# A four-layer graph network on one core: the edge grid of the preparing stage goes from 125 partitions of 800 steps to 128 partitions of 784 steps

## The chip, the cores and the metric

One Trainium2 chip, of which the kernel uses one core. The core has five engines: TensorE (PE; its weight loads are listed as PEld), VectorE (DVE), ScalarE (ACT), GpSimd (POOL) and SyncE (SP), each with an instruction queue of its own, and 16 DMA engines that all queues share. The engines meet through semaphores only. The metric is the device time of one execution in microseconds (us); lower is better.

## The reference, cut to what matters

There are 6250 nodes with 256 features and 100,000 edges. Each edge has a source, a destination, a type, a weight and a row of 128 attributes. The edges are given in order of destination. Four layers follow each other, each on the layer-normalised rows of the one before, each added to the running x:

```python
h = relu(layernorm(x)); x = x + L0(h, src, dst, edge_weight, ...)   # segment sum over src of (h@W)[dst]*weight
h = relu(layernorm(x)); x = x + L1(h, edge_index, edge_attr, ...)   # segment sum over src of edge_attr@W, in and out degrees
h = relu(layernorm(x)); x = x + L2(h, edge_index, edge_weight, ...) # attention over the edges of each dst, then a feed-forward
h = relu(layernorm(x)); x = x + L3(h, ..., src, dst, edge_type)     # segment sum over dst, then a GRU cell
```

So the edges are needed once grouped by source (layers 0 and 1) and once grouped by destination (layers 2 and 3).

## The kernel before

The kernel runs stages one after the other: `prepare`, `source_sums`, `layers_0_and_1`, `attention`, `layer_2`, `relations_and_layer_3`. Only `prepare` is touched by the change. The later stages walk over tiles of 128 edges of a sorted list; for each of 832 tiles GpSimd gathers 128 rows of a DRAM table with an indirect DMA (lines 782, 1289 and 1905).

`prepare` sorts. It lays the edges out as a grid of `EP` partitions by `STEPS` steps (125 by 800, which is exactly 100,000). What it does, engine by engine:

- VectorE ranks the edges by the block of 128 nodes to which their source belongs (`rank("src")`): it counts each of 49 blocks over the whole grid (line 554), then walks through the grid in four segments of `SEG` = 200 steps and writes each edge's place in the sorted list into `pos_src` (lines 572, 577, 583, 587). When a segment is done it raises `ranked_steps`. Then come the row statistics of x, a wait for GpSimd's `rstd` (line 663), the table of the tiles by source, the same ranking by destination, and the one-hots for the in-degrees (lines 689 and 691, a pair for each of the 800 steps), which TensorE sums (line 513). Its work on the grid ends with the copy of line 698.
- SyncE loads the edge attributes into `rec`, 8 steps (`HALF`) of all partitions at a time. `rec` has two halves, and half `h` is loaded again only when all 8 scatters out of it have landed (`rec_stored[h]`).
- ScalarE completes a half: it waits for the load (`rec_loaded[h]`) and the ranking, copies 8 columns of places into `pos_slot` (line 477) and four more fields into the records (line 478), and raises `rec_ready`.
- GpSimd writes the sorted records to DRAM: for each step one indirect DMA (a scatter, line 410) that takes one record of 132 floats (528 bytes) from each partition and writes it to the row of `src_records` that `pos_slot` names. So there is one scatter for each of the `STEPS`, 8 for a half, 16 for a turn of the loop. After the first 12 turns (`FIRST_PAIR`) GpSimd computes `rstd` (line 421), for which VectorE waits.

```python
gp.indirect_dma_start(out=src_records,
                      out_offset=bass.IndirectOffsetOnAxis(ap=pos_slot[:, k:k + 1], axis=0),
                      in_=rec[:, k, :], in_offset=None).then_inc(rec_stored[h], 16)
```

After its last scatter GpSimd waits until all have landed, copies the fields of the edges to DRAM tables (line 452), gathers them in windows of 128 (line 464), and `prepare` ends; `source_sums` begins with reading `src_records`.

Of the kernel before, what the change touches and what calls it, by code (L numbers as in the profile page):

```python
# [14 lines left out]
F32 = mybir.dt.float32  # L15
BF16 = mybir.dt.bfloat16
I32 = mybir.dt.int32
# [7 lines left out]
P = 128  # L25
NODES, D = 6250, 256
EDGES, ED = 100000, 128
BLOCKS = -(-NODES // P)
NODES_PAD = BLOCKS * P
LAST_ROWS = NODES - (BLOCKS - 1) * P  # L30
EP = 125
STEPS = EDGES // EP
UNROLL = 8
# [10 lines left out]
REC = ED + 4  # L44
# [127 lines left out]
def build(nc, A, OUT):  # L172
    with ExitStack() as whole:
# [20 lines left out]
        src_records = dram("src_records", (EDGES + P, REC))  # L194
        by_dst = {n: dram(f"by_dst_{n}", (EDGES + P, 1), F32 if n == "wgt" else I32)
# [31 lines left out]
def prepare(env):  # L227
# [3 lines left out]
    HALF = 8  # L231
    SEG = STEPS // 4
    SB = TURN_BLOCKS
    PAIRS = (BLOCKS - 1) // 2
    FIRST_PAIR = 12
    REC_TURNS = STEPS // (2 * HALF)
    with nc.cleanup_on_exit(), ExitStack() as ctx:
# [22 lines left out]
        iota_i = sb(ctx, "iota_i", [P, P], I32)  # L260
        pidx_i = sb(ctx, "pidx_i", [P, 1], I32)
# [66 lines left out]
        rel_pad = sem("x_pad")  # L328

        def grid(ap):  # L330
            return ap.rearrange("(p t) -> p t", t=STEPS)
# [3 lines left out]
        with nc.Block() as block:  # L335
            @block.sync
            def _(sp):
                sp.dma_start(key["src"][:], grid(A["src"])).then_inc(loaded_src, 16)
                sp.dma_start(key["dst"][:], grid(A["dst"])).then_inc(loaded_rest, 16)
                sp.dma_start(wgt[:], grid(A["edge_weight"])).then_inc(loaded_rest, 16)  # L340
                sp.dma_start(typ[:], grid(A["edge_type_16"])).then_inc(loaded_rest, 16)
                sp.dma_start(pair[:], A["dst"][STEPS - 1:STEPS - 1 + (EP - 1) * STEPS]
                             .rearrange("(p t) -> p t", t=STEPS)[:, 0:2]).then_inc(loaded_rest, 16)

                attr = A["edge_attr_128"].rearrange("(p t) d -> p t d", t=STEPS)

                def load(turn, h):
                    sp.dma_start(rec[:, h * HALF:(h + 1) * HALF, 0:ED],
                                 attr[:, bass.ds(turn * 2 * HALF + h * HALF, HALF), :]
                                 ).then_inc(rec_loaded[h], 16)  # L350

                for h in range(2):
                    load(0, h)
# [33 lines left out]
            def _(gp):  # L387
# [10 lines left out]
                gp.wait_ge(iotas, 7)  # L398
                nc.gpsimd.memset(ones_row[:], 1.0).then_inc(tail_ready, 1)
                gp.wait_ge(loaded_rest, 64)  # L400
# [56 lines left out]
                for ch in range(CHUNKS):  # L457
                    if ch:
                        gp.wait_ge(win_cast, ch)
                    for n, name in enumerate(("src", "dst", "wgt", "typ")):  # L460
                        w = windows[:, n, :]
                        if name == "wgt":
                            w = w.bitcast(F32)
                        gp.indirect_dma_start(out=w, out_offset=None, in_=by_dst[name],
                                              in_offset=bass.IndirectOffsetOnAxis(ap=start_i["dst"][:, ch:ch + 1], axis=0)
                                              ).then_inc(win_loaded, 16)

            @block.scalar
            def _(ac):

                def complete(turn):
# [15 lines left out]
                with ac.Fori(0, FIRST_PAIR) as turn:  # L487
                    complete(turn)
                ac.wait_ge(rstd_ready, 2)
                ac.wait_ge(loaded_x, 32)  # L490
                with ac.Fori(0, PAIRS) as pair_i:
                    complete(pair_i + FIRST_PAIR)
                    normalise(pair_i * 2)
                    normalise(pair_i * 2 + 1)
                normalise(BLOCKS - 1)
                with ac.Fori(FIRST_PAIR + PAIRS, REC_TURNS) as turn:
                    complete(turn)
# [30 lines left out]
            def _(ve):  # L528
                d = Counter(ve, dve)
                nc.vector.memset(X[:, BLOCKS - 1, :], 0.0).then_inc(rel_pad, 1)  # L530
# [10 lines left out]
                def rank(side, hi_t):  # L541

                    if side == "dst":
                        ve.wait_ge(loaded_rest, 64)
                    else:
                        ve.wait_ge(loaded_src, 16)
# [102 lines left out]

                ve.wait_ge(tail_ready, 2)  # L650
# [1487 lines left out]
```

## Time and profile before

| | us |
|---|---|
| median of 3 runs (5604.88 to 5611.56) | 5610.76 |
| the profiled execution, its device time | 5615.93 |
| its span from the first to the last instruction | 5614.1 |
| GpSimd's first scatter starts | 115.3 |
| GpSimd's last scatter starts | 1379.3 |
| VectorE's last operation on the grid starts | 1040.4 |
| first tile gather of the next stage starts | 1497.0 |

The span is the profiler's; the device time lies 1.8 us above it. Times in the rows further down are us from the span's start, and durations of single instructions are in ns where the row says so. "Idle before" a group is the time its engine stood still just before instructions of that group, with what ended it; "issue" means that nothing which the profile shows was waited for.

### The profile page before, as it was taken

The numbers are of one execution on the slowest core, as the hardware profiler recorded it, in microseconds if no ns is written. First come the engines' busy times: TensorE is split into PE (matmuls) and PEld (weight loads), VectorE is DVE, ScalarE is ACT, GpSimd is POOL, SyncE is SP. The second block draws the span as 40 slices with busy tenths as digits, with TensorE's granted clock in tenths as the row PEclk, the third lists the DMA queues.
The fourth block names the chain that finished last, engine by engine and source line by source line (L and its number), as shares of the span: only waits on it lengthen the run. The fifth ranks groups of instructions, "written<-read, shape, count | busy, mean of one in ns | idle before, by whom it ended". The sixth has DMA issues, their size and how long they took to land. (4 is left out here: it accounts for less than half of the span.)

```text
span 5614.1 us, 108115 instructions
## 1 busy us (share of the span) xinstructions
PE 3530.3 (63%) x16558; PEld 2634.7 (47%) x16559; DVE 3950.7 (70%) x14077; ACT 1757.7 (31%) x6303; POOL 3898.1 (69%) x4332
## 2 busy tenths in 40 slices
PE   0000035200277777776768999999989778888887
PEld 0000012100255555554547888888879644554444
DVE  9918999300477777774568888888868766666665
ACT  0000000000133333332337777777756411111111
POOL 2878887776477777775766666666647777676774
PEclk9999999999999999997879999999999889899998
DMA  2232233335355555554323333333322233333332
GB/s 75 76 84 79 76 82 88 87 88 125 76 156 157 157 158 155 157 157 93 94 86 96 94 94 94 95 94 95 94 66 66 88 111 114 103 110 106 108 108 78
DMA packets 491102, 578.41 MB, mean 103 GB/s; under 512 B 114758, under 2 KB 394328, under 8 KB 490945
## 3 DMA queue, kind: packets, MB, share of 16 engines
q0 software_dynamic: 189536, 397.34, 25.4%
q1 hardware_dynamic: 301473, 180.10, 11.8%
q14 instruction: 67, 0.55, 0.0%
q8 instruction: 26, 0.43, 0.0%
HBM read 491.28 MB, written 86.57 MB: 103 GB/s over the span
## 5 line engine op out<-in xcount | busy, mean ns | idle before, releaser
L410 POOL DMA_INDIRECT src_records<-rec,pos_slot x800 | 1005.0, 1256 | 345.2 <-issue 237.0
L1289 POOL DMA_INDIRECT a_row<-h_rows,a_idx x832 | 787.6, 947 | 369.8 <-PE a_p_s L1415 197.1
L1905 POOL DMA_INDIRECT r_row<-h_rows,r_idx x832 | 802.1, 964 | 310.2 <-issue 168.2
L782 POOL DMA_INDIRECT s_row<-h_rows,s_idx x832 | 794.5, 955 | 299.7 <-issue 171.7
L794 PE MATMUL s_sums<-s_row,s_hotw 128*128 128x256 f32 x1664 | 584.9, 434 | 329.8 <-DMA s_row<-h_rows,s_idx 231.7
L1946 PE MATMUL r_p_s<-r_row,r_hot 128*128 128x272 f32 x1664 | 602.2, 474 | 233.2 <-DVE r_row L2080 215.1
L1392 PE MATMUL a_p_q<-nodes,a_hotT 128*128 x1664 | 569.8, 424 | 55.5 <-DVE a_score L1459 54.1
L1946 PEld LDWEIGHTS r_p_s<-r_row,r_hot 128*128 128x128 f32 x1664 | 335.4, 221 | 516.8 <-DVE r_row L2080 233.8
L820 DVE TENSOR_TENSOR nodes<-nodes,s_sums 128x385 f32 x832 | 461.5, 555 | 157.1 <-PE s_sums L795 138.7
L1415 PE MATMUL a_p_s<-a_row,a_masked 128*128 128x257 f32 x1664 | 497.0, 380 | 2.1 <-DVE sums L1496 1.4
L794 PEld LDWEIGHTS s_sums<-s_row,s_hotw 128*128 128x128 f32 x1664 | 253.0, 192 | 477.1 <-issue 369.6
L2088 DVE TENSOR_TENSOR sums<-sums,r_p_s 128x272 f32 x832 | 358.6, 431 | 149.3 <-PE r_p_s L1946 103.2
L773 ACT ACTIVATE s_idx<-s_rec 128x1 int32<-128x1 f32 x832 | 167.9, 202 | 863.3 <-DMA s_rec<-src_records 731.3
L1496 DVE SCALAR_TENSOR_TENSOR sums<-sums,a_fade,a_p_s 128x257 f32 x832 | 399.3, 480 | 41.7 <-PE a_p_s L1415 3.7
L1459 DVE CUSTOM_DVE_ANT_0 a_prod<-a_p_q,a_row 128x258 f32<-128x258 f32 x832 | 353.5, 425 | 104.9 <-ACT a_masked L1338 63.3
L795 PEld LDWEIGHTS s_sums<-s_rec,s_hot 128*128 128x128 f32 x1664 | 323.0, 194 | 46.1
L477 ACT ACTIVATE pos_slot<-pos_src 125x8 int32 x100 | 20.9, 209 | 1014.8 <-DMA rec<-in_edge_attr 991.4
L1415 PEld LDWEIGHTS a_p_s<-a_row,a_masked 128*128 128x128 f32 x1664 | 314.5, 190 | 49.5 <-ACT a_masked L1359 2.3
L795 PE MATMUL s_sums<-s_rec,s_hot 128*128 128x129 f32 x1664 | 326.2, 278 | 0.0
L1338 ACT ACTIVATE a_masked<-a_far,a_score 128x128 f32<-128x128 f32 x832 | 323.7, 389 | 2.0 <-DVE a_score L1459 2.0
L1359 ACT ACTIVATE a_masked<-a_masked,a_mneg 128x128 f32<-128x128 f32 x832 | 324.2, 390 | 0.0
L504 PE MATMUL p_total<-cnt,ones 125*128 125x49 f32 x4 | 1.3, 432 | 492.2 <-DVEq L559 492.2
(308 smaller groups left out, 8747.5 us busy)
## 6 DMA issues: line engine op xcount, KB each, us to landing
s_rec<-src_records SPq DMA_DIRECT2D x832, 66.0 KB
rec<-in_edge_attr SPq DMA_DIRECT2D x100, 500.0 KB
s_row<-h_rows,s_idx POOLq DMA_INDIRECT x832
a_row<-h_rows,a_idx POOLq DMA_INDIRECT x832, 2.8
r_row<-h_rows,r_idx POOLq DMA_INDIRECT x832, 2.8
src_records<-rec,pos_slot POOLq DMA_INDIRECT x800
h_rows<-H SPq DMA_DIRECT2D x1, 6272.0 KB
x_rows<-nodes SPq DMA_DIRECT2D x49, 128.0 KB, 1.9
```

The costliest lines, as they stand in the source:

```text
L410: gp.indirect_dma_start(out=src_records, out_offset=bass.IndirectOffsetOnAxis(ap=pos_slot[:, k:k + 1], axis=0), in_=rec[:, k, :], in_offse ...
L782: gp.indirect_dma_start(out=row[:, k, :], out_offset=None, in_=env["h0_rows"], in_offset=bass.IndirectOffsetOnAxis(ap=idx[:, k:k + 1], axis=0)
L794: nc.tensor.matmul(sums[k % 4][:, 0:D], hotw[:, k, :], row[:, k, :], start=True, stop=True)
L795: nc.tensor.matmul(sums[k % 4][:, D:NW], hot[:, k, :], rec[:, k, 0:ED + 1], start=True, stop=True).then_inc(summed, 1)
L820: nc.vector.tensor_tensor(s, s, sums[k % 4][:, 0:NW].rearrange("p (a b) -> p a b", a=1), ALU.add).then_inc(added, 1)
L1289: gp.indirect_dma_start(out=row[:, k, 0:D], out_offset=None, in_=env["h2_rows"], in_offset=bass.IndirectOffsetOnAxis(ap=idx[:, k:k + 1], a ...
L1392: nc.tensor.matmul(p_q[k % 2], hotT[:, k % F, :], query[:, bass.ds(b, 1), 0:RW].rearrange("p a d -> p (a d)"), start=True, stop=True).then ...
L1415: nc.tensor.matmul(p_s[k % 2], masked[:, k % F, :], row[:, k, 0:D + 1], start=True, stop=True).then_inc(S["summed"], 1)
L1496: nc.vector.scalar_tensor_tensor(out=s, in0=s, scalar=fade[:, k % F:k % F + 1], in1=p_s[k % 2], op0=ALU.mult, op1=ALU.add).then_inc(S["add ...
L1905: gp.indirect_dma_start(out=row[:, k % R, 0:D], out_offset=None, in_=env["h3_rows"], in_offset=bass.IndirectOffsetOnAxis(ap=idx[:, k:k + 1 ...
L1946: nc.tensor.matmul(p_s[k % 4], hot[:, k % H, :], row[:, k % R, :], start=True, stop=True).then_inc(S["summed"], 1)
L2088: nc.vector.tensor_tensor(s, s, p_s[k % 4], ALU.add).then_inc(S["added"], 1)
```

## The change

The grid is now 128 partitions of 784 steps. The first 127 partitions are full (99,568 edges), the last one holds the remaining 432 and has 352 spare cells. The spare cells get a key that belongs to no block, a place beyond the table's used part (`spare_i`, rows 100,128 and up of a `src_records` that is 352 rows longer), and are scattered there. All loops over steps run 784 times, a segment is 196 steps, and there are 49 turns of 16 instead of 50. A grid can no longer be loaded with one DMA, so each load becomes one of 112 partitions, one of 15, and one of the last partition where that still has edges (its 432 steps are 27 turns).

```diff
-EP = 125
-STEPS = EDGES // EP
+EP = 128
+STEPS = -(-EDGES // (EP * 16)) * 16
+LAST_STEPS = EDGES - (EP - 1) * STEPS
+SPARE = STEPS - LAST_STEPS
+FULL = 112
...
+    LAST_TURNS = LAST_STEPS // (2 * HALF)
+    LOADS_SRC, LOADS_REST = 3 * 16, (3 * 3 + 2) * 16
...
+        def load_grid(sp, t, ap, done):
+            for a, b in ((0, FULL), (FULL, EP - 1)):
+                sp.dma_start(t[a:b, :], ap[a * STEPS:b * STEPS].rearrange("(p t) -> p t", t=STEPS)).then_inc(done, 16)
+            sp.dma_start(t[EP - 1:EP, 0:LAST_STEPS], ap[(EP - 1) * STEPS:EDGES].rearrange("(p t) -> p t", p=1)).then_inc(done, 16)
...
-                sp.dma_start(key["src"][:], grid(A["src"])).then_inc(loaded_src, 16)
+                sp.wait_ge(spare_set, 1)
+                load_grid(sp, key["src"], A["src"], loaded_src)
+                sp.wait_ge(spare_set, 4)
+                load_grid(sp, key["dst"], A["dst"], loaded_rest)
...
-                def load(turn, h):
-                    sp.dma_start(rec[:, h * HALF:(h + 1) * HALF, 0:ED],
-                                 attr[:, bass.ds(turn * 2 * HALF + h * HALF, HALF), :]
-                                 ).then_inc(rec_loaded[h], 16)
+                def load(turn, h, last):
+                    steps = bass.ds(turn * 2 * HALF + h * HALF, HALF)
+                    ks = slice(h * HALF, (h + 1) * HALF)
+                    sp.dma_start(rec[0:FULL, ks, 0:ED], rows[0][:, steps, :]).then_inc(rec_loaded[h], 16)
+                    sp.dma_start(rec[FULL:EP - 1, ks, 0:ED], rows[1][:, steps, :]).then_inc(rec_loaded[h], 16)
+                    if last:
+                        sp.dma_start(rec[EP - 1:EP, ks, 0:ED], rows[2][:, steps, :]).then_inc(rec_loaded[h], 16)
...
-                with sp.Fori(1, REC_TURNS) as turn:
+                with sp.Fori(1, LAST_TURNS) as turn:
                     for h in range(2):
-
                         sp.wait_ge(rec_stored[h], turn * (16 * HALF))
-                        load(turn, h)
+                        load(turn, h, True)
+                with sp.Fori(LAST_TURNS, REC_TURNS) as turn:
+                    for h in range(2):
+                        sp.wait_ge(rec_stored[h], turn * (16 * HALF))
+                        load(turn, h, False)
...
+                nc.gpsimd.iota(spare_i[:], [[1, SPARE]], base=EDGES + P, channel_multiplier=0).then_inc(iotas, 1)
...
-                        ac.wait_ge(rec_loaded[h], turn * 16 + 16)
+                        if last:
+                            ac.wait_ge(rec_loaded[h], turn * 48 + 48)
+                        else:
+                            ac.wait_ge(rec_loaded[h], turn * 32 + (LAST_TURNS * 16 + 32))
...
+                for t, value in ((key["src"], NODES_PAD), (key["dst"], NODES_PAD), (wgt, 0.0), (typ, 0)):
+                    nc.vector.memset(t[96:EP, LAST_STEPS:STEPS], value).then_inc(spare_set, 1)
...
+                ve.wait_ge(iotas, 8)
+                for side in ("src", "dst"):
+                    nc.vector.tensor_copy(pos[side][:, LAST_STEPS:STEPS], spare_i[:]).then_inc(spare_placed, 1)
+                ve.wait_ge(spare_placed, 2)
```

SyncE's queue, the loop that loads `rec` from the second turn on, before the change (a row is one instruction; its shape is partitions x steps x floats):

```order
L358 ISA
L348 ISA
L348 DMA rec<-in_edge_attr 125x8x128
L348 ISA
L348 DMA rec<-in_edge_attr 125x8x128
L358 REGISTER_ALU
L358 COMPARE_AND_BRANCH
```

The same place after the change, the first of the two loops (turns 1 to 26, in which the last partition still has edges):

```order
L377 ISA
L366 ISA
L366 DMA rec<-in_edge_attr 112x8x128
L367 ISA
L367 DMA rec<-in_edge_attr 15x8x128
L369 ISA
L369 DMA rec<-in_edge_attr 1x8x128
L366 ISA
L366 DMA rec<-in_edge_attr 112x8x128
L367 ISA
L367 DMA rec<-in_edge_attr 15x8x128
```

Where one DMA stood for a half there are now three; the second loop (turns 27 to 48) has the first two of them only. GpSimd's loop has the same instructions as before, 8 scatters for a half, in fewer turns and on 128 partitions.

## Rows read from the trace of the kernel before

**Rows 1.** The page, its head.
```profile
span 5614.1 us, 108115 instructions
```

**Rows 2.** Engines by stage (windows): `prepare`'s scatters, the stage behind.
```profile
core 0: us, PE busy (x) PEld busy (x) DVE busy (x) ACT busy (x) POOL busy (x), PEclk, DMA share, GB/s
115.00:1381.00 1266.00, 158.74 (x806) 82.78 (x806) 773.71 (x3233) 73.17 (x256) 1013.21 (x801) 1.00 0.32 85
...
1490.00:2570.00 1080.00, 767.35 (x3328) 574.12 (x3328) 840.89 (x2498) 330.13 (x1664) 794.48 (x832) 0.98 0.57 153
```

**Rows 3.** Waits of 100 to 1365 us: total us, times, longest.
```profile
ACT pos_slot L477 <- DMA rec<-in_edge_attr: 980.5, 85, 21.0
...
DVE nmr L663 <- POOL rstd L421: 126.2, 1, 126.2
```

**Rows 4.** Groups of GpSimd instructions over the span: busy us, mean ns, idle before.
```profile
L410 POOL DMA_INDIRECT src_records<-rec,pos_slot x800 | 1005.0, 1256 | 345.2 <-issue 237.0 <-ACTq L480 108.2
...
L782 POOL DMA_INDIRECT s_row<-h_rows,s_idx x832 | 794.5, 955 | 299.7 <-issue 171.7 <-ACT s_idx L773 128.0
...
L464 POOL DMA_INDIRECT windows<-by_dst_dst,start_i_dst x7 | 6.6, 947 | 2.1 <-issue 2.1
```

**Rows 5.** Views of lines 410 and 782: ns min/median/max, first and last start.
```profile
L410 POOL DMA_INDIRECT src_records<-rec,pos_slot x800: 1182/1187/3593, 115.3 to 1379.3; - x160
...
L782 POOL DMA_INDIRECT s_row<-h_rows,s_idx x832: 940/946/1056, 1497.0 to 2562.0; - x167
```

**Rows 6.** Line 410 alone by stretch: length, POOL busy (x count), clock, DMA.
```profile
115.30:427.26 311.96, 248.05 (x192) 1.00 0.30 79
437.43:1031.00 593.57, 479.19 (x374) 1.00 0.31 82
1031.00:1380.50 349.50, 277.73 (x234) 1.00 0.36 96
```

**Rows 7.** Timeline from 1200 us: start, length, instruction, idle before.
```profile
1199.99 1.19 POOL L410 DMA_INDIRECT src_records<-rec,pos_slot  x1 [0.30 <-issue]
...
1203.55 48.13 SPq L348 DMA_DIRECT2D rec<-in_edge_attr  x5
...
1212.28 0.21 ACT L477 ACTIVATE pos_slot<-pos_src 125x8 int32 x1 [12.84 <-DMA rec<-in_edge_attr]
...
1213.56 1.19 POOL L410 DMA_INDIRECT src_records<-rec,pos_slot  x1 [0.45 <-issue]
```

**Rows 8.** DMA view, 1200 to 1300 us: packets, queues, issues.
```profile
DMA packets 13400, 8.60 MB, mean 86 GB/s; under 512 B 4060, under 2 KB 12395, under 8 KB 13400
...
q0 software_dynamic: 5360, 4.50, 17.9%
q1 hardware_dynamic: 8040, 4.10, 14.4%
...
src_records<-rec,pos_slot POOLq DMA_INDIRECT x67
```

**Rows 9.** DMA view, 1600 to 1700 us, the stage behind.
```profile
DMA packets 14846, 15.47 MB, mean 155 GB/s; under 512 B 2482, under 2 KB 12344, under 8 KB 14846
...
q0 software_dynamic: 3750, 10.25, 33.7%
...
s_row<-h_rows,s_idx POOLq DMA_INDIRECT x79
```

**Rows 10.** DMA view, 1205 to 1208 us, inside one load of `rec`.
```profile
q1 hardware_dynamic: 480, 0.25, 27.2%
```

**Rows 11.** Timeline of GpSimd around `rstd`.
```profile
427.26 8.24 POOL L421 TENSOR_TENSOR rstd<-vare,half 128x49 f32<-128x49 f32 x1
437.43 1.27 POOL L410 DMA_INDIRECT src_records<-rec,pos_slot  x1 [1.92 <-ACTq L480]
```

**Rows 12.** View of line 698, VectorE's last grid operation.
```profile
L698 DVE COPY indeg<-p_deg x1: 211/211/211, 1040.4 to 1040.4; 128x49 f32<-128x49 f32 x1
```

**Rows 13.** Timeline behind the last scatter, GpSimd's first table copy.
```profile
1389.79 0.58 POOL L452 DMA_DIRECT2D by_dst_src<-in_src  x1 [9.31 <-issue]
```

More of the change, by code:

```diff
@@ L193, in build @@
         h0_rows = dram("h0_rows", (NODES_PAD, D))
-        src_records = dram("src_records", (EDGES + P, REC))
-        by_dst = {n: dram(f"by_dst_{n}", (EDGES + P, 1), F32 if n == "wgt" else I32)
+        src_records = dram("src_records", (EDGES + P + SPARE, REC))
+        by_dst = {n: dram(f"by_dst_{n}", (EDGES + P + SPARE, 1), F32 if n == "wgt" else I32)
                   for n in ("src", "dst", "wgt", "typ")}
@@ L260, in prepare @@
         iota_i = sb(ctx, "iota_i", [P, P], I32)
+        spare_i = sb(ctx, "spare_i", [P, SPARE], I32)
         pidx_i = sb(ctx, "pidx_i", [P, 1], I32)
@@ L328, in prepare @@
         rel_pad = sem("x_pad")
-        def grid(ap):
-            return ap.rearrange("(p t) -> p t", t=STEPS)
+        spare_set, spare_placed = sem("spare_set"), sem("spare_placed")
+        def load_grid(sp, t, ap, done):
+            for a, b in ((0, FULL), (FULL, EP - 1)):
+                sp.dma_start(t[a:b, :], ap[a * STEPS:b * STEPS].rearrange("(p t) -> p t", t=STEPS)).then_inc(done, 16)
+            sp.dma_start(t[EP - 1:EP, 0:LAST_STEPS], ap[(EP - 1) * STEPS:EDGES].rearrange("(p t) -> p t", p=1)).then_inc(done, 16)
         nfull = (BLOCKS - 1) * P
@@ L337, in _ @@
             def _(sp):
-                sp.dma_start(key["src"][:], grid(A["src"])).then_inc(loaded_src, 16)
[L339 to L342, printed above, removed]
-                             .rearrange("(p t) -> p t", t=STEPS)[:, 0:2]).then_inc(loaded_rest, 16)
@@ new lines, in _ @@
+                load_grid(sp, wgt, A["edge_weight"], loaded_rest)
+                load_grid(sp, typ, A["edge_type_16"], loaded_rest)
+                sp.dma_start(pair[0:EP - 2, :], A["dst"][STEPS - 1:STEPS - 1 + (EP - 2) * STEPS]
+                             .rearrange("(p t) -> p t", t=STEPS)[:, 0:2]).then_inc(loaded_rest, 16)
+                sp.dma_start(pair[EP - 2:EP - 1, :], A["dst"][(EP - 1) * STEPS - 1:(EP - 1) * STEPS + 1]
+                             .rearrange("(p t) -> p t", p=1)).then_inc(loaded_rest, 16)
@@ new lines, in _ @@
+                attr = A["edge_attr_128"]
+                rows = [attr[a * STEPS:b * STEPS, :].rearrange("(p t) d -> p t d", t=STEPS) for a, b in ((0, FULL), (FULL, EP - 1))]
+                rows.append(attr[(EP - 1) * STEPS:EDGES, :].rearrange("(p t) d -> p t d", p=1))
+                def load(turn, h, last):
[5 more added lines that the diff above has]
+                        sp.dma_start(rec[EP - 1:EP, ks, 0:ED], rows[2][:, steps, :]).then_inc(rec_loaded[h], 16)
@@ L352, in _ @@
                 for h in range(2):
-                    load(0, h)
+                    load(0, h, True)
                 sp.wait_ge(rel_pad, 1)
@@ L463, in _ @@
                             w = w.bitcast(F32)
-                        gp.indirect_dma_start(out=w, out_offset=None, in_=by_dst[name],
+                        gp.indirect_dma_start(out=w, out_offset=None, in_=by_dst[name][0:EDGES + P, :],
                                               in_offset=bass.IndirectOffsetOnAxis(ap=start_i["dst"][:, ch:ch + 1], axis=0)
@@ L469, in _, with complete @@
             def _(ac):
-                def complete(turn):
+                def complete(turn, last):
                     for h in range(2):
@@ L487, in _ @@
                 with ac.Fori(0, FIRST_PAIR) as turn:
-                    complete(turn)
+                    complete(turn, True)
                 ac.wait_ge(rstd_ready, 2)
                 ac.wait_ge(loaded_x, 32)
-                with ac.Fori(0, PAIRS) as pair_i:
-                    complete(pair_i + FIRST_PAIR)
+                ALL_LAST = LAST_TURNS - FIRST_PAIR
+                with ac.Fori(0, ALL_LAST) as pair_i:
+                    complete(pair_i + FIRST_PAIR, True)
+                    normalise(pair_i * 2)
+                    normalise(pair_i * 2 + 1)
+                with ac.Fori(ALL_LAST, PAIRS) as pair_i:
+                    complete(pair_i + FIRST_PAIR, False)
                     normalise(pair_i * 2)
@@ L496, in _ @@
                 with ac.Fori(FIRST_PAIR + PAIRS, REC_TURNS) as turn:
-                    complete(turn)
+                    complete(turn, False)
             @block.tensor
```

10 lines of the change are left out of this document (5 added, 5 removed).

## The prediction

> **What bounds the kernel now.** I read the page first, then the busy time of the engines by stage. The stage that the change touches is `prepare`, and the stretch that counts in it is the one of the scatters. It is 1266 us of the span's 5614.1, and in it GpSimd is busy for 1013 us [rows 1, 2]. Nothing in it overlaps with the next stage, which reads the finished `src_records`; so a microsecond off the last scatter is a microsecond off the end, as long as GpSimd stays what ends last.
>
> That it does is to be seen in two steps. VectorE's last operation on the grid starts at 1040.4, 340 us before the last scatter is issued [rows 5, 12]. And GpSimd's own idle time is 345 us in 800 scatters, of which 237 are the 0.30 us between one DMA instruction and the next; 108 are waits for ScalarE, nearly all of them the one wait before the first scatter, which starts at 115.3 [rows 4, 5]. ScalarE's long waits for the loads, 980 us, are those of an engine with nothing to do [rows 3]. But the loads have little room. In the timeline the last scatter of a half ends at 1201.18 (1199.99 + 1.19), SyncE issues that half's next load at 1203.55, ScalarE sees it at 1212.28, and GpSimd starts on it at 1213.56 with 0.45 us of idle time in place of 0.30 [rows 7]. This loop took 12.38 us; the other half's 8 scatters cover 8 x 1.49 + 0.30 = 12.2. So GpSimd binds, with the load loop right behind.
>
> **What a scatter costs, and on what.** A scatter of 125 records takes 1.187 us in the median, a gather of 128 rows 0.946, with the same 0.30 us between instructions [rows 4, 5]. Fewer rows take longer, so the count of rows does not set the price. The gather's row length does not either: the windows of 512-byte rows take 0.947, the rows of 1024 bytes 0.955 in the mean [rows 4]. The DMA view shows what differs. In 100 us there are 67 scatters with 5360 packets on the software queue: 80 for each, and about 60 of these 80 are under 512 bytes (4060, less the 40 or so that end 8 loads), so 20 carry records [rows 8]. 80 is 16 rings of 5 packets. 125 is not a multiple of 16, and it looks as if 5 rings got 25 records each (in 4 packets, and one that signals), while the other 11 rings were filled with small packets to the same length. A gather has 3750/79 = 47.5, say 48 packets, 3 for each ring, and the only small ones are those that signal [rows 9]: 8 rows on each of 16 rings. The loads tell the same: while one runs, it keeps 27.2% of the 16 DMA engines busy, 4.4 of them, never more than 5 [rows 10]. I read it so: GpSimd writes as many entries on every ring as the fullest has, 25 now, 8 with 128 partitions. Then (1.187 - 0.946)/17 = 14 ns for an entry on all rings.
>
> The Trainium skill ("DMA: Bandwidth & Descriptors", section on why a DMA increments its semaphore by 16) gives the rule: the number of engines is the largest up to 16 that divides the partitions, which makes 5 of 125 and 16 of 112 and of 128. The trace agrees. The same section has an exception that speaks against this change: some direct software copies are spread over all 16 with the partitions divided and rounded up, and by that 125 would already lie on 16 rings. The 80 packets speak against it here; with it, a scatter would have some 32.
>
> **The change part by part.**
>
> *The scatter's price.* From 1.187 to 0.946, so -0.241 us each. The bounds: 0.940, the gather's least, and 1.187 x 128/125 = 1.216, if rows set the price after all. I take the gather's, because the packets say that the new scatter has the gather's layout.
>
> *First 192 scatters* (12 turns, the same count): 311.96/192 = 1.625 us now, of which 1.292 busy, so 0.105 above the median from waits for VectorE [rows 6]. I leave that share as it is: 192 x 1.384 = 265.7, -46.2 us. `rstd` and the start after it stay at 10.2 us [rows 11]: GpSimd goes on at 391. VectorE, which waits 126 us for `rstd` [rows 3], goes on 46 us earlier.
>
> *Until VectorE is done.* VectorE needed 605 us from there to 1040.4 [rows 3, 12]. A fiftieth of its steps goes, 12 us at most; I take 9. It ends at about 985. GpSimd's rate beside it was 593.57/374 = 1.587, now 1.346: 441 scatters until 985.
>
> *After it.* 592 - 441 = 151 scatters are left, at 349.50/234 = 1.494 less 0.241, so 189 us. The last one ends at 1174, before at 1380.5: **-206 us**. The 16 scatters that are gone are in this sum; they are 25 us of it (16 x 1.555, all stages [rows 4]).
>
> *The loads.* An issue more or two for each half, on SyncE, which waits nearly always; each 0.3 us or so. The records themselves come over 16 engines in place of 5, so the 5 to 6 us that a load now takes to flow fall to about 2. From the loop's 12.38 I take 3.5 off for the data and put 0.6 on for the issues, 9.5 us; the new cover is 8 x 1.246 + 0.30 = 10.3. It stays hidden, with 0.8 us of room. Bounds: 8.5, and the present 12.38, which would no longer be hidden (see the rivals).
>
> *Front and back.* Four memsets and two copies on VectorE and an iota on GpSimd before the first ranking, 2 us at most, against 1 us each from shorter counts and a first segment of 196 steps, and a key load that is spread wider: nothing, within 2 us. Behind the last scatter GpSimd waits 9.3 us before its table copies [rows 13], while SyncE writes `h0_rows`, which starts one turn before the end. A turn is shorter by 16 x 0.241 = 3.9 us, so this write reaches up to that much further past the end: I take +3.
>
> Sum: 5615.93 - 206 + 3 = 5413 for the profiled execution's kind. That one lies 5.2 us above the median, so **5408**.
>
> **The rivals.**
>
> *The load loop takes over.* The loads keep their 12.38 us: what they wait for is then the landing of writes and not the data, and three DMAs end later than one. Then a turn is 12.38 + 8 scatters. In the three stages a half would take 0.6, 0.7 and 1.2 us more than above; times 24, 55 and 19 halves that is 14 + 38 + 23 = 75 us: 5483. Near it in price is a lockstep: VectorE's passes hold GpSimd up in its rank phases (1.29 against 1.187 busy [rows 6]), and a shorter scatter may just wait longer. Against both: ScalarE found the load ready 1 us earlier in the other half, and the load's data do take half of the loop.
>
> *The scatter keeps its price*: a scatter costs more than a gather because it writes to DRAM rows, not because of the rings. Then only the 16 scatters go, -25, and up to 0.029 x 784 = 23 come back if rows count: 5586 to 5609, in the middle 5595. For it: the trace has no scatter on 128 partitions. The exception of the Trainium skill (the same section as above) would lead to this case too.
>
> *Slower.* What a scatter has above a gather, 0.241 us, is a price for each ring that carries records, paid on the write side: 5 now, 16 then. That is 0.048 for a ring, +0.53 us each, 784 x 0.53 - 25 = +390: 6000. It turns to a loss from a scatter of about 1.22 us on: 800 x 1.555 = 784 x (1.22 + 0.30 + 0.07). Against it: the gathers use 16 rings at 0.946, and their signals go to 16 rings as well.
>
> **How the numbers follow.** The forecast 0.70, its own range 5370 to 5450 (the upper end a load loop or a waiting GpSimd that takes back 0.4 us in a half, the lower end fewer waits for VectorE, since the 0.1 us of them should shrink with the entries written). A part given back (5450 to 5530) 0.11. The price kept 0.13, of which a quarter within 0.2% of 5610.8 (11 us, about what a measurement of this kernel can tell from no change). Slower 0.06. The range must leave out no more than 0.2: from 5370 it reaches through the second case and up to half of the third, 5592. Faster 0.90, same 0.04, slower 0.06.
>
> **What would show it.** In the new profile: a median scatter near 0.95 us; 48 or fewer packets for each, none small but the signals; the load at well over 5 engines' share; `rstd` at about 381, VectorE's last grid operation near 985, the last scatter near 1173; GpSimd's idle time still mostly the 0.30 us. A median near 1.19 makes the forecast wrong at its main step; idle time for ScalarE of 30 us or more beyond the first wait shows the load loop. The later stages should keep their lengths, the next one its 1080 us [rows 2].

## The result and the profile after

The kernel with the change takes **5395.23 us** in the median (5393.96 to 5396.02, 4 runs) against 5611.16 for the kernel before on the same chip (5604.88 to 5616.32, 4 runs): a ratio of **0.9615**, interval 0.9599 to 0.9632. That is 216 us less. The profiled execution spans 5392.2 us, 221.9 less than the one of before [rows 1].

The views of the two scattered and gathered lines come first (ns min/median/max, first and last start; they answer to [rows 5]), then line 735, VectorE's last grid operation [rows 12]:
```profile
L433 POOL DMA_INDIRECT src_records<-rec,pos_slot x784: 963/969/2642, 112.3 to 1161.0; - x196
  issue: 241.5, 763
  ACTq L506: 103.7, 21
```
```profile
L819 POOL DMA_INDIRECT s_row<-h_rows,s_idx x832: 940/946/1067, 1277.9 to 2341.9; - x167
```
```profile
L735 DVE COPY indeg<-p_deg x1: 210/210/210, 966.8 to 966.8; 128x49 f32<-128x49 f32 x1
```
The scatter's median fell from 1.187 to 0.969 us. The last one starts at 1161.0 in place of 1379.3, and the first gather of the next stage at 1277.9 in place of 1497.0: 219 us earlier, nearly the whole of the gain. That stage takes as long as it did, 1064 us from its first to its last gather against 1065. GpSimd's idle time stayed what it was, 345 us, of which 241.5 are the 0.30 us between instructions.

The same stretches as in [rows 6], line 433 alone (length, busy and count, clock, DMA share, GB/s):
```profile
112.30:367.40 255.10, 195.38 (x192) 1.00 0.36 98
377.45:966.80 589.35, 449.65 (x440) 1.00 0.36 98
966.80:1162.00 195.20, 147.32 (x153) 1.00 0.44 124
```
And two views of the DMA queues, of 1050 to 1150 us (for [rows 8]) and of one microsecond within a load (for [rows 10]):
```profile
DMA packets 13989, 11.46 MB, mean 115 GB/s; under 512 B 1515, under 2 KB 12777, under 8 KB 13989
...
q1 hardware_dynamic: 11572, 6.33, 25.3%
q0 software_dynamic: 2417, 5.12, 16.4%
...
src_records<-rec,pos_slot POOLq DMA_INDIRECT x79
```
```profile
q1 hardware_dynamic: 509, 0.25, 97.9%
```
A scatter now makes 2417/79 = 30.6 packets, where it made 80 (the probe of the first experiment, with nothing cut off by the window's edges, has 256 for 8 scatters of 128 rows, 32 each). Half of them carry records, and the rest are those that signal. A load keeps 97.9% of the 16 engines busy in that microsecond; before, it was 27.2% in the mean over three microseconds, and 33.7% in the fullest single microsecond of 1204 to 1209.

In the timeline the load loop can be read beside [rows 7]:
```profile
1049.01 0.97 POOL L433 DMA_INDIRECT src_records<-rec,pos_slot  x1 [0.30 <-issue]
...
1051.47 0.32 SPq L366 DMA_DIRECT2D rec<-in_edge_attr  x1
...
1051.98 0.43 SPq L367 DMA_DIRECT2D rec<-in_edge_attr  x1
...
1056.67 0.21 ACT L503 ACTIVATE pos_slot<-pos_src 128x8 int32 x1 [10.20 <-DMA rec<-in_edge_attr]
...
1060.46 0.97 POOL L433 DMA_INDIRECT src_records<-rec,pos_slot  x1 [0.30 <-issue]
```
ScalarE sees a load 5.2 us after its issue; it saw it after 8.7. The last scatter of the half that is loaded again ends at 1049.98 (1049.01 + 0.97). SyncE issues the load 1.5 us after that (2.4 before), ScalarE has it at 1056.67 and hands it on some 1.2 us later (1.15 in `rings_only` below, 1120.81 - 1119.66), 7.8 us in all. GpSimd comes back to this half at 1060.46, 10.5 us after it left it; that is the cover. No scatter waits for a load here.

### The profile page after: what moved, and what is told of

Read it like the earlier page. It is cut to its first block and busy times, and to the rows that moved or that the text cites. A ratio compares the mean times of both kernels' runs of the same rounds, so it can differ in the third digit from the quotient of the medians.

```text
span 5392.2 us, 108399 instructions
## 1 busy us (share of the span) xinstructions
PE 3534.7 (66%) x16542; PEld 2630.4 (49%) x16543; DVE 3921.8 (73%) x14051; ACT 1755.2 (33%) x6299; POOL 3696.6 (69%) x4317
## 5 line engine op out<-in xcount | busy, mean ns | idle before, releaser
L433 POOL DMA_INDIRECT src_records<-rec,pos_slot x784 | 792.3, 1011 | 345.1 <-issue 241.5
L848 DVE TENSOR_SCALAR s_hot<-iota,s_loc 128x128 f32<-128x128 f32 x832 | 239.5, 288 | 78.7 <-ACT s_loc L811 74.2
L503 ACT ACTIVATE pos_slot<-pos_src 128x8 int32 x98 | 20.4, 209 | 834.2 <-DMA rec<-in_edge_attr 811.5
```

The costliest lines, as they stand in the source:

```text
L433: gp.indirect_dma_start(out=src_records, out_offset=bass.IndirectOffsetOnAxis(ap=pos_slot[:, k:k + 1], axis=0), in_=rec[:, k, :], in_offse ...
```

## The experiments

The kernel before takes 5611 us on the chip of the first four experiments and about 7,000 us on those of the others, in every run on them; a time is therefore compared only with those of the same set of runs, and every ratio is against the kernel before on the same chip. The four were run together on one chip, where the kernel before took 5611.74 us (5605.52 to 5617.48, 13 runs).

**1. `forms`: what sets the price.** Behind the last scatter of the changed kernel stand eleven groups of 8 scatters into a spare tensor, and five of 8 gathers from `src_records`. One group is shown, with N for its number of rows; each group reads columns of `probe_i` of its own:
```diff
+for k in range(8):
+    gp.indirect_dma_start(out=probe_d, out_offset=bass.IndirectOffsetOnAxis(ap=probe_i[0:N, 8 + k:8 + k + 1], axis=0),
+                          in_=rec[0:N, k, :], in_offset=None).then_inc(probe_s, 16)
+own_wait(gp, probe_s, 256)
...
```


> The changed kernel with a probe behind its last scatter, while VectorE is idle: eleven groups of 8 scatters with 128, 127, 126, 125, 124, 120, 112, 100, 96, 64 and 16 partitions to a table of their own, then five groups of 8 gathers with 128, 127, 125, 112 and 16 partitions. Nothing of the result is left out. Ring theory (the price follows the entries on the fullest ring; rings = largest number up to 16 that divides the partitions): 0.87 us + 0.0128 us per entry, from 0.969 at 8 and 1.187 at 25 entries. So 0.97 (128), 2.5 (127: one ring), 0.98 (126: 14 rings of 9), 1.19 (125), 1.26 (124: 4 rings of 31), 0.97 (120), 0.96 (112), 0.99 (100: 10 of 10), 0.94 (96), 0.92 (64), 0.88 (16); gathers the same less 0.02, so a gather of 125 about 1.16. Direction theory (a scatter to DRAM rows costs more than a gather): scatter 125 about 1.19, gather 125 about 0.95. Row theory with a penalty for any count that is no multiple of 16: 127, 126, 125, 124, 120 and 100 all about 1.19, and 127 no dearer than 125.

Measured, in one run (5631.80 us). Four of the gathers and three of the scatters, in the groups by line (busy us, mean ns; N is 127 on lines 459 and 492, 124 on 468, 125 on 465 and 495, 128 on 489, 16 on 501):
```profile
L459 POOL DMA_INDIRECT probe_d<-rec,probe_i x8 | 20.4, 2545 | 23.3 <-DMA probe_d<-rec,probe_i 15.7 <-issue 7.6
L492 POOL DMA_INDIRECT rec<-src_records,probe_i x8 | 20.4, 2545 | 10.4 <-issue 7.9 <-DMA rec<-src_records,probe_i 2.5
L468 POOL DMA_INDIRECT probe_d<-rec,probe_i x8 | 10.5, 1312 | 5.1 <-DMA probe_d<-rec,probe_i 3.0 <-issue 2.1
L495 POOL DMA_INDIRECT rec<-src_records,probe_i x8 | 9.6, 1203 | 8.5 <-DMA rec<-src_records,probe_i 6.4 <-issue 2.1
L465 POOL DMA_INDIRECT probe_d<-rec,probe_i x8 | 9.4, 1178 | 4.5 <-DMA probe_d<-rec,probe_i 2.4 <-issue 2.1
...
L489 POOL DMA_INDIRECT rec<-src_records,probe_i x8 | 7.6, 952 | 6.7 <-issue 4.8 <-DMA probe_d<-rec,probe_i 1.9
...
L501 POOL DMA_INDIRECT rec<-src_records,probe_i x8 | 6.7, 840 | 4.4 <-DMA rec<-src_records,probe_i 2.3 <-issue 2.1
```
The medians of all scatters, beside the records on the fullest ring if the number of rings is the largest up to 16 that divides the rows:

| rows | 128 | 127 | 126 | 125 | 124 | 120 | 112 | 100 | 96 | 64 | 16 |
|---|---|---|---|---|---|---|---|---|---|---|---|
| rings | 16 | 1 | 14 | 5 | 4 | 15 | 16 | 10 | 16 | 16 | 16 |
| fullest | 8 | 127 | 9 | 25 | 31 | 8 | 7 | 10 | 6 | 4 | 1 |
| ns | 958 | 2542 | 978 | 1178 | 1311 | 986 | 934 | 980 | 912 | 897 | 836 |

127 rows cost 2.54 us and 128 cost 0.96; the price follows the third line and not the first. From 8 to 127 on the fullest ring it is (2542 - 958)/119 = 13.3 ns for one more, in the mean. It is not a perfect line: 124 rows lie 47 ns above it (expected 1.26 us, measured 1.31), and 120 rows cost 28 ns more than 128 with the same 8 on the fullest ring.

That the other rings are filled to the length of the fullest is in the packets of this trace: the 8 gathers of 127 rows (1356.8 to 1391.4 us), then the software queue at the 8 scatters of 127 (1195.6 to 1229.0):
```profile
DMA packets 2176, 0.60 MB, mean 17 GB/s; under 512 B 2048, under 2 KB 2048, under 8 KB 2176
```
```profile
q0 software_dynamic: 2176, 0.60, 11.3%
```
These are 272 packets for each, 17 on each of 16 rings, of which only 16, the packets of one ring, carry rows; the other 256 are small. 125 and 124 rows both make 80 packets and yet cost 1.18 and 1.31 us, so the price goes by the entries on the fullest ring and not by the packets. A gather of 125 rows takes 1.20 us as a scatter of 125 does, so the direction sets nothing. What falls: that rows set the price, and that a write to DRAM does. The Trainium skill ("DMA: Bandwidth & Descriptors", section on why a DMA increments its semaphore by 16) names one engine for 127 partitions and sixteen for 128; the two prices bear it out for indirect software copies, which do not take that section's exception.

**2 to 4. The parts of the change apart.** `rings_only` is the kernel before, with 125 partitions of 800 steps, in which the scatter is widened to 128 partitions; the three spare ones write their rows behind the edges. ScalarE's two copies for a half widen with it, and `spare_i` takes room among the buffers. The loads stay as they were.
```diff
-meta = sb(ctx, "meta", [EP, STEPS, 4])
-rec = sb(ctx, "rec", [EP, 2 * HALF, REC])
-pos_slot = sb(ctx, "pos_slot", [EP, 2 * HALF], I32)
+meta = sb(ctx, "meta", [P, STEPS, 4])
+rec = sb(ctx, "rec", [P, 2 * HALF, REC])
+pos_slot = sb(ctx, "pos_slot", [P, 2 * HALF], I32)
...
+nc.gpsimd.iota(spare_i[:], [[1, STEPS]], base=EDGES + P - 125 * STEPS, channel_multiplier=STEPS).then_inc(spare_set, 1)
...
+nc.vector.memset(rec[96:P, :, :], 0.0).then_inc(rec_set, 1)
+nc.vector.memset(meta[96:P, :, :], 0.0).then_inc(meta_set, 1)
...
+nc.vector.tensor_copy(pos["src"][96:P, :], spare_i[96:P, :]).then_inc(spare_placed, 1)
```


> The kernel before, still 125 x 800 and with its one load per half on 125 partitions, but each scatter goes out of all 128 partitions: the three spare ones send zeros to spare rows. Ring theory: a median scatter of 0.97 us in place of 1.187. But the load now has only 8 x 1.27 = 10.2 us of cover for a loop of about 12 us, so GpSimd should wait about 1 us in each half: 100 halves of 11.1 to 11.4 us, 5470 to 5500 us in all. If the loads stay hidden even so: 5416 (the changed kernel's 5395 and 16 more scatters of 1.33 us). Rival (the gain is that of fewer steps or of the grid, not of the rings): scatters of 1.19 us, 5600 us.

`rings_split` has this and each load of `rec` in two, of 112 and 13 partitions; `split_only` is the kernel before with nothing but that split.
```diff
-sp.dma_start(rec[:, h * HALF:(h + 1) * HALF, 0:ED],
-             attr[:, bass.ds(turn * 2 * HALF + h * HALF, HALF), :]
-             ).then_inc(rec_loaded[h], 16)
+for a, b in ((0, 112), (112, EP)):
+    sp.dma_start(rec[a:b, h * HALF:(h + 1) * HALF, 0:ED],
+                 attr[a:b, bass.ds(turn * 2 * HALF + h * HALF, HALF), :]
+                 ).then_inc(rec_loaded[h], 16)
...
-ac.wait_ge(rec_loaded[h], turn * 16 + 16)
+ac.wait_ge(rec_loaded[h], turn * 32 + 32)
```


> As the last one, but each load is split into 112 and 13 partitions. If both parts of my theory hold (the scatter's rings set its price, the loads' width keeps them hidden), this is the changed kernel with 16 more scatters: 5395 + 16 x 1.33 = 5416 us, and 50 to 80 us less than the one with the old loads. If the loads don't matter, the two are the same within 5 us.

> The kernel before with nothing changed but its loads, split into 112 and 13 partitions. The loads were nearly hidden: GpSimd's waits for ScalarE beyond the first were 15 us. Theory: 5596 to 5611 us, scatters at 1.187 us as before. Rival (wide loads free the DMA engines and make the scatters faster by themselves): under 5570 us.

Measured; the groups of the scatter follow, in this order:

| kernel | us | ratio | interval |
|---|---|---|---|
| `rings_only` | 5453.18 | 0.9719 | 0.9703 to 0.9735 |
| `rings_split` | 5412.81 | 0.9646 | 0.9630 to 0.9662 |
| `split_only` | 5607.60 | 0.9993 | 0.9983 to 1.0002 |

```profile
L415 POOL DMA_INDIRECT src_records<-rec,pos_slot x800 | 807.6, 1010 | 390.3 <-issue 245.5 <-ACTq L485 144.8
```
```profile
L416 POOL DMA_INDIRECT src_records<-rec,pos_slot x800 | 807.7, 1010 | 350.0 <-issue 247.7 <-ACTq L486 102.3
```
```profile
L411 POOL DMA_INDIRECT src_records<-rec,pos_slot x800 | 1005.2, 1257 | 337.0 <-issue 238.3 <-ACTq L481 98.7
```
The wide scatter alone is worth 158.6 us (5611.74 - 5453.18). With it the loads on 5 engines come out of hiding: ScalarE is waited for 42.5 us longer than with split loads (144.8 - 102.3), and the time is 40 us more. Both are less than expected: `rings_only` lies 17 us below its range of 5470 to 5500, and 50 to 80 us were expected between the two. Without the wide scatter the split is worth nothing that can be told, 4 us. So the wide loads gain nothing by themselves and keep 40 us of what the wide scatter gains. What is left between `rings_split` and the changed kernel is 17.6 us (5412.81 - 5395.23, each from its own set of runs): in the spans it is 19.9 us. Of these the first scatter's earlier start is 5.3 (117.6 to 112.3) and the stretch from the first to the last scatter 22.2, nearly all of it the 16 scatters fewer at 1.340 us from one to the next; the later stages give 2.0. Behind the last scatter the changed kernel loses 9.6 us, since it needs 116.9 us until the next stage's first gather where `rings_split` needs 107.3.

In the timeline of `rings_only` the narrow load shows at one half in two, once a turn of 21.38 us (1099.43 to 1120.81), where 16 scatters take 20.4:
```profile
1099.43 0.96 POOL L415 DMA_INDIRECT src_records<-rec,pos_slot  x1 [1.16 <-ACTq L485]
...
1119.66 0.21 ACT L482 ACTIVATE pos_slot<-pos_src 128x8 int32 x1 [11.43 <-DMA rec<-in_edge_attr]
...
1120.81 0.97 POOL L415 DMA_INDIRECT src_records<-rec,pos_slot  x1 [1.32 <-ACTq L485]
```

**5 to 7. Other chip: the change again, one long load, `h0_rows` in pieces.** These three were run together on a chip where the kernel before took 7003.65 us (6983.97 to 7023.98). `after_again` is the changed kernel as it stands. `one_load` loads 127 partitions at once in place of 112 and 15:
```diff
-sp.dma_start(rec[0:FULL, ks, 0:ED], rows[0][:, steps, :]).then_inc(rec_loaded[h], 16)
-sp.dma_start(rec[FULL:EP - 1, ks, 0:ED], rows[1][:, steps, :]).then_inc(rec_loaded[h], 16)
+sp.dma_start(rec[0:EP - 1, ks, 0:ED], whole[:, steps, :]).then_inc(rec_loaded[h], 16)
...
```
and `h_pieces` writes `h0_rows` in 13 pieces, one in each of the last 12 turns and one behind them, in place of one write of 6.3 MB:
```diff
+with sp.Fori(REC_TURNS - 12, REC_TURNS) as turn:
+    for h in range(2):
+        sp.wait_ge(rec_stored[h], turn * (16 * HALF))
+        load(turn, h, False)
+    part = bass.ds((turn - (REC_TURNS - 12)) * 4, 4)
+    sp.dma_start(h0_out[:, part, :], H[:, part, :]).then_inc(h0_stored, 16)
+sp.dma_start(h0_out[:, 48:49, :], H[:, 48:49, :]).then_inc(h0_stored, 16)
-sp.dma_start(env["h0_rows"].rearrange("(i p) d -> p i d", p=P), H[:]).then_inc(h0_stored, 16)
...
```


> The changed kernel itself, beside the others of this job: 5395 us, within 3.

> The changed kernel with the first two DMAs of each load (112 and 15 partitions) made one of 127; nothing is left out. 127 has no divisor up to 16 but 1. Ring theory: the load runs on one DMA engine, 1016 pieces of 512 bytes at the 28 ns that a piece takes now, 28.5 us, and with 6 us around it the load loop is 35 us. A turn is then 35 + 8 x 1.27 = 45 us in place of 21, 49 turns: about 1150 us more, 6550 us, with GpSimd idle for more than half of the stretch; the scatters keep 0.97 us. Rival (the split of the loads was not needed): 5395 us.

> The changed kernel, with the 6.3 MB write of the normalised rows (h0_rows) taken out of its place behind the last load and sent in 12 pieces of 4 blocks, one in each of the last 12 turns, and the last block behind them. In the changed kernel's trace the four table copies after the last scatter take 31 us to land, behind this write. Theory: they then land in 8 to 12 us and start 3 us earlier, 5370 us. Rival (the pieces delay the loads in the same rings, or the copies are slow by themselves): 5390 to 5400 us.

Measured: `after_again` **7196.16** us, ratio **1.0288** (1.0247 to 1.0328): slower here, not faster. `h_pieces` 7159.59, ratio 1.0218 (1.0182 to 1.0254). Its median lies 37 us below that of `after_again`, but its runs (7149.08 to 7193.96) and those of `after_again` (7154.93 to 7218.02) overlap, so this difference alone shows nothing. `one_load` 8300.69, one run; its scatter group, and one half in its timeline:
```profile
L434 POOL DMA_INDIRECT src_records<-rec,pos_slot x784 | 775.2, 989 | 1918.3 <-ACTq L507 1697.6 <-issue 220.6
```
```profile
1494.96 26.30 SPq L370 DMA_DIRECT2D rec<-in_edge_attr  x1
...
1498.26 0.21 ACT L504 ACTIVATE pos_slot<-pos_src 128x8 int32 x1 [25.32 <-DMA rec<-in_edge_attr]
...
1499.43 0.97 POOL L434 DMA_INDIRECT src_records<-rec,pos_slot  x1 [17.18 <-ACTq L507]
...
1526.10 0.96 POOL L434 DMA_INDIRECT src_records<-rec,pos_slot  x1 [16.79 <-ACTq L507]
```
The scatter itself is as quick as before. A half takes 26.7 us (1526.10 - 1499.43), no more than the 26.30 us of its one load and a gap, and a turn 53.3 where 45 was expected: the loads of the two halves do not run beside each other but one behind the other, as they would on one engine. The split into 112 and 15 is what the layout of 127 full partitions needs.

**8 to 10. Why slower there.** On another chip (the kernel before 6986.71 us, 6970.20 to 7019.60) the kernel before (`before_again`), the changed kernel (`after_third`) and `h_pieces` (`h_pieces_again`) ran together, the first for its trace.

> The kernel before itself, for its trace on the chip of this job. In the last job its runs took 7004 us and the changed kernel's 7196, with the same scatters of 0.97 us in the changed kernel; VectorE stood still for hundreds of us in its ranking loops with nothing that the profile shows as the cause, and ended its grid work at 1592 us, behind the last scatter. If this job's chip is like the first two, 5611 us and VectorE's last grid operation at 1040; if it is like the last one, this trace shows whether VectorE is the bound of the preparing stage there before the change too.

> The changed kernel once more: 5395 us, ratio 0.9615, on a chip like the first; about 1.03 on one like the last.

> The pieces again, beside the changed kernel: 5370 us on a chip like the first, 25 us below it, because the four table copies no longer stand behind the 6.3 MB write. In the last job the two stood 37 us apart, in the same direction. Rival: no difference beyond 5 us where VectorE doesn't bind.

Measured: `before_again` 6992.95 us (one run); `after_third` 7196.09 us, ratio **1.0317** (1.0280 to 1.0355); `h_pieces_again` 7144.56, ratio 1.0230 (1.0213 to 1.0247), 52 us less, and here the runs do not overlap (7140.85 to 7156.03 against 7161.48 to 7220.35). The scatters and VectorE's last grid operation, first of the kernel before, then of the changed one:
```profile
L410 POOL DMA_INDIRECT src_records<-rec,pos_slot x800: 1183/1190/3591, 115.3 to 1378.8; - x160
...
L698 DVE COPY indeg<-p_deg x1: 209/209/209, 1307.3 to 1307.3; 128x49 f32<-128x49 f32 x1
```
```profile
L433 POOL DMA_INDIRECT src_records<-rec,pos_slot x784: 964/972/3193, 112.4 to 1292.4; - x196
...
L735 DVE COPY indeg<-p_deg x1: 210/210/210, 1588.6 to 1588.6; 128x49 f32<-128x49 f32 x1
```
The scatter has its gain there too: 1.190 to 0.972 us, and the last one starts 86 us earlier. But VectorE, which in the kernel before had 340 us of room on the first chip and has 71.5 on this one, now ends 281 us later than in the kernel before, and 296 us behind the last scatter. The end of `prepare` waits for it. GpSimd's waits there, 60 to 1610 us, have it in two places (total us, times, longest), behind the last scatter and ahead of `rstd`:
```profile
POOL windows L487 <- DVE windows_f L744: 257.3, 2, 254.8
...
POOL rstd L444 <- DVE vare L172: 50.2, 1, 50.2
```
In the kernel before the first of these waits is 5.4 us at the longest, and the second does not occur. The second, with 42 us more of waiting for ScalarE (145.4 against 103.7), is also why the last scatter starts at 1292.4 here and at 1161.0 on the first chip: VectorE's slow ranking already holds the scatters up. The next stage's first gather starts at 1658.2, against 1491.6, and these 166.6 us are all but 2 of the 168.6 by which the two spans differ (7159.7 and 6991.1; the traced run of the changed kernel is the shortest of its four).

The traces of `h_pieces` show nothing gained in `prepare`. The four table copies land sooner in `h_pieces_again` (GpSimd waits 8.9 us for them in place of 27.1), but they start later (18.9 us of waiting in place of 7.4), and VectorE ends last all the same, at 1590.7 against 1588.6; the next stage's first gather starts at 1660.2 against 1658.2. The 52 us are therefore not the effect that was expected; where they come from stays open.

What VectorE does in that time is in its waits of the changed kernel there, 60 to 1610 us (total us, times, longest), and in a few rows of its timeline:
```profile
DVE cum_seg L610 <- issue: 200.1, 104, 3.7
DVE pos_dst L616 <- issue: 166.4, 80, 7.4
```
```profile
905.16 0.62 DVE L610 TENSOR_TENSOR_SCAN cum_seg<-ones_row,base,eq 128x196 f32<-128x196 bf16 x1 [2.39 <-issue]
906.57 0.39 DVE L605 TENSOR_SCALAR eq<-hi_d,iota 128x196 uint16<-128x196 bf16 x1 [0.78 <-issue]
907.98 0.38 DVE L616 COPY_PREDICATED pos_dst<-eq,cum_seg 128x196 f32<-128x196 uint16 x1 [1.02 <-issue]
908.26 0.15 DVE L620 TENSOR_SCALAR base<-cum_seg 128x1 f32 x1
```
The operations have their lengths, but before three in four stands idle time for nothing that the profile shows (for a smaller part of it, 39.1 us of `pos_src` and 34.5 of `pos_dst`, the profile names a queue that it does not know, which it does in `prepare` in no trace from the first chip and in none of the kernel before): a block of the ranking takes 5.6 us there (905.16 to 910.78 for the next scan) and 1.1 us in the changed kernel's trace on the first chip. The stretches of all engines tell when. The changed kernel at three places (length; PE, PEld, DVE, ACT, POOL busy and counts):
```profile
800.00:900.00 100.00, 0.00 (x0) 0.00 (x0) 21.05 (x69) 7.88 (x26) 73.03 (x74) 1.00 0.34 99
...
1100.00:1200.00 100.00, 0.00 (x0) 0.00 (x0) 20.30 (x60) 2.95 (x18) 75.17 (x77) 1.00 0.36 103
...
1400.00:1500.00 100.00, 62.56 (x281) 29.34 (x281) 93.88 (x561) 0.00 (x0) 0.00 (x0) 1.00 0.00 0
```
and the kernel before on that chip:
```profile
600.00:700.00 100.00, 0.00 (x0) 0.00 (x0) 98.07 (x345) 7.03 (x24) 81.20 (x60) 1.00 0.29 78
...
1000.00:1100.00 100.00, 31.33 (x143) 14.83 (x143) 62.12 (x287) 5.31 (x21) 79.56 (x68) 1.00 0.33 89
```
In the changed kernel VectorE stands still beside the scatters, during the ranking (21 us of work in 100), and is at its pace of the first chip once they are over. The kernel before does the ranking undisturbed beside its scatters (98 in 100) and loses time in the one-hot loop (62 in 100, where it has 95 on the first chip). TensorE's granted clock stands at 1.00 in all five rows, so it is not what differs here.

**11 and 12. Wide loads or wide scatters?** On a fourth chip (the kernel before 6989.66 us, 6956.45 to 7006.70, 9 runs) `split_again` is `split_only` once more and `rings_again` is `rings_only`.

> The kernel before with only its loads split into 112 and 13 partitions, once more, for a chip on which the kernel before takes 7000 us. There the changed kernel's VectorE stood still in its ranking loops (last grid operation at 1589 us) and that of the kernel before did not until 722 us (last one at 1307). VectorE's instructions are the same in this kernel as before, not one is moved. Theory of the wide loads (bursts on all 16 DMA engines get in the way of what feeds VectorE its instructions): VectorE's ranking of the sources stretches as in the changed kernel, its last grid operation comes at 1450 us or later, and the kernel takes 7100 us or more. Theory of the moved code (the six more instructions ahead of VectorE's loops shift them): ranking as before, 1307 us, 7000 us. On a chip like the first: 5608 us, and nothing is told apart.

> The kernel before with scatters on 128 partitions and its narrow loads (5 DMA engines), once more, for a chip on which the kernel before takes 7000 us. Theory of the wide loads: VectorE's ranking is as before (scan passes end at 722 us or sooner) and its last grid operation near 1300 us; 6900 to 7000 us. Theory that wide scatters do it: ranking stretches, 1450 us or later, 7100 us or more. Theory of the moved code: it may stretch here too, since three instructions were added ahead of the loops; then only the kernel with split loads tells. On a chip like the first: 5453 us.

Measured: `split_again` 6980.14 us, ratio 0.9994 (0.9971 to 1.0017); `rings_again` **7249.61** (2 runs, 7249.48 and 7249.75), ratio **1.0359** (1.0329 to 1.0389). The same two lines of each, `split_again` first:
```profile
L411 POOL DMA_INDIRECT src_records<-rec,pos_slot x800: 1182/1187/3591, 115.2 to 1371.4; - x160
...
L699 DVE COPY indeg<-p_deg x1: 209/209/209, 1329.9 to 1329.9; 128x49 f32<-128x49 f32 x1
```
```profile
L415 POOL DMA_INDIRECT src_records<-rec,pos_slot x800: 962/969/1486, 117.6 to 1293.3; - x160
...
L708 DVE COPY indeg<-p_deg x1: 211/211/211, 1698.6 to 1698.6; 128x49 f32<-128x49 f32 x1
```
The wide loads cause none of it. The narrow loads with the wide scatter have all of it, and more: VectorE ends 369 us later than in `split_again`. `rings_only` differs from the kernel before in the scatter, in ScalarE's copies that widen with it, in three more instructions on VectorE ahead of its loops (two waits come with the last), and in one buffer more, `spare_i`; the runs do not tell these apart.

## Why the prediction was right, and where not

The time, 5395.23 us, lies in the likeliest case's own range, 13 us below the forecast. The mechanism was right; that the forecast lies so near is in part luck, since two sizes were off by 18 and 29 us in opposite directions. By the prediction's steps:

- **The ring reading**, the step that all else hangs on, is shown twice: by the packets (32 in place of 80, and 272 at 127 rows), and by the prices of eleven widths. The 14 ns for an entry measured 13.3. One reading on the way was too strong: [rows 10] gives a mean of 4.4 engines and not "never more than 5"; single microseconds reach 33.7%, which would be 5.4.
- **The scatter's price** was put at the gather's 0.946 and is 0.969: 0.023 x 784 = 18 us too little. The probe's scatter of 128 rows took 0.960 in the mean against 0.952 for a gather, behind the last scatter, where VectorE is not ranking; so part of the 0.023 is the place, and the rest is open.
- **The waits for VectorE** were left as they were, and they halved. That they are waits for VectorE was not tested; what the rows show is that the scatters are longer only while VectorE works (behind it the mean is 277.73/234 = 1.187 before and 147.32/153 = 0.963 after). Busy time above the median was 0.105 us in the first stretch and 0.094 in the second [rows 6]; it is 195.38/192 - 0.969 = 0.049 and 449.65/440 - 0.969 = 0.053. That is -11 and -18 us. The text had it as the reason for its lower end.
- **The stretches.** `rstd` starts at 367.4 (381 foreseen: 3 us from an earlier start, 11 from the above), VectorE ends at 966.8 (985). From there to the last scatter 153 were left (151), at 195.20/153 = 1.276 (1.253). The last scatter starts at 1161.0 (near 1173).
- **The loads** stay hidden: a loop of 7.8 us (9.5 foreseen) against a cover of 10.5 (10.3). From issue to ScalarE it is 3.5 us less, the extra issues included, where 2.9 were foreseen, and the scatters land 0.9 us sooner, which was put at nothing. The rival that they take over was right about the mechanism and wrong about the case: `rings_only`, which leaves the loads on 5 engines, loses 40 us to them, against 75 for that rival (70 or 82 by its own numbers, as the 0.30 us of the cover is counted or not). ScalarE sees a load in 5.2 us in place of 8.7, so what it waited for was the data.
- **Front and back** were put at 0 and +3 us. The first scatter starts 3.0 us earlier (112.3), and from the last scatter's end to the next stage it is 115.9 against 116.5. In that, the table copies land 3.4 us later (30.6 us of waiting against 27.2), as the +3 had it, but the wait ahead of them is 2.1 shorter (7.2 against 9.3) and those between the gathers of windows 1.9. Whether the write of `h0_rows` is what the copies wait for was tried only on the chips of 7,000 us, where VectorE ends last; there GpSimd waited 6 and 18 us less for the copies with the write in pieces, and `prepare` gained nothing by it. On the first chip it wasn't measured.
- **Scatter keeps its price** and **slower for each ring that carries records**: both fall. The scatter went down by 0.218 us where rings with records went from 5 to 16.

The sum: -3 at the start, -56.9 until `rstd`, -158.6 from there to the last scatter's end, -0.6 behind it, -2.8 in the later stages, together the -221.9 of the spans (-206 + 3 was said; the profiled run of the kernel before lies 5 us above its median and that of the changed kernel 1 below, which is why the medians differ by 216).

**What the prediction doesn't cover** is the other chips. On three on which the kernel before takes 7,000 us, the change, or the wide scatter alone, makes the time 2.9 to 3.6% longer, in 3 sets of runs. The scatter is as much cheaper there; VectorE, which the prediction rightly saw 340 us ahead, becomes what ends last. That this decides is shown by GpSimd's wait of 254.8 us for it. Why VectorE stands still is not shown. What is shown: it goes with the wide scatter or with what was added beside it (three instructions on VectorE, wider copies on ScalarE, one buffer more), not with the split loads; it happens while scatters run, and stops with them. A repeat of the kernel before with only those additions and the narrow scatter would tell, and wasn't run.

## What to carry to other kernels

Look at the packets of an indirect copy before counting its rows: 125 rows cost more than 128, and 127 cost 2.7 times as much, since all 16 rings are filled to the length of the fullest; choose widths that 16 divides, even with idle rows. Widen what feeds it along with it, or the gain is partly lost to the load that was just hidden. And measure a change on more than one chip before keeping it: here an engine with 340 us of room on one was the bound on three others, and the sign turned.

## What was not expected

- A load of 127 partitions takes 26.3 us for 8 steps, and the two halves' loads queue behind each other (8300.69 us for the kernel).
- The same kernel takes 5611 us on one chip and 6987 to 7004 on three. Over the whole span the mean granted TensorE clock is 0.955 of full speed in the trace of before on the first chip and 0.858 on the third; whether that is a cause of the longer time or follows from it is open. In the stage behind `prepare` the gathers have the same length (median 0.946 and 0.949 us) but are 1597 us apart from first to last in place of 1065 (1491.6 to 3088.8 in the trace of before on the third chip).
- On those chips VectorE has idle time ahead of its instructions, beside GpSimd's scatters, for nothing that the profile shows. Which of its loops meets it differs from kernel to kernel: the one-hot loop in the kernel before, the ranking in the changed one.
